# GpSimd's program order in a six-stage decoder kernel: when it issues scatters, triangle masks and normalisation steps

## What is computed

```python
x = _layernorm(x + _L0_attn_ref(x, ...))        # stage 1: linear attention by cumulative sums
x = _layernorm(x + _L0_xattn_ref(x, ctx, mask)) # stage 2: cross attention over 512 context tokens
x = _layernorm(x + _L0_ffn_ref(x, ...))         # stage 3: top-2 of 8 experts, sparse deltas on W
x = _layernorm(x + _L1_attn_ref(x, ...))        # stage 4: sliding window attention, 32 heads
x = _layernorm(x + _L1_xattn_ref(x, ctx, ...))  # stage 5: quantised cross attention, 16 heads
x = _layernorm(x + _L1_ffn_ref(x, ...))         # stage 6: top-6 of 64 experts
```

```python
rows = mask_idx // H
cols = mask_idx % H
vals = jnp.einsum('tk,tks->ts', rw, weighted[top_idx])
contrib = jax.ops.segment_sum((xg * vals).T, rows, num_segments=H)
out = xt @ W.T + contrib.T
```

## Time and profile before

| | |
|---|---|
| runs of the kernel | 472.28, 475.8 and 476.39 us, median 475.8 |
| profiled execution, span from first to last instruction | 473.8 us |
| TensorE matmuls busy | 388.1 us, 82% of the span |
| VectorE busy | 303.7 us, 64% |
| ScalarE busy | 215.5 us, 45% |
| GpSimd busy | 118.4 us, 25% |
| mean granted TensorE clock | 0.879 of full speed |

### The profile page before, as it was taken

The page is one execution under the profiler, slowest core; times in us unless marked ns, Lnnn a source line. Parts: engine busy times, 40 slices in busy tenths (PEclk is TensorE's granted clock), DMA queues, the critical chain, the costliest instruction groups (busy, mean ns, idle before and its releaser), DMA issues.

```text
span 473.8 us, 6810 instructions
## 1 busy us (share of the span) xinstructions
PE 388.1 (82%) x2387; PEld 225.7 (48%) x2387; DVE 303.7 (64%) x611; ACT 215.5 (45%) x551; POOL 118.4 (25%) x215
## 2 busy tenths in 40 slices
PE   5996969389987999999754867768676998999993
PEld 2645457244434566576532223333344544665572
DVE  4984498959624697878646979989871362132235
ACT  2664221272235765855214789899881311111100
POOL 8248646828460000000080111212110000000002
PEclk9989895779988899999985589998975698999997
DMA  8992110670000000000000999999982004011211
GB/s 244 318 361 25 1 2 1 223 310 1 0 1 0 1 3 0 2 1 1 2 0 13 265 169 172 155 163 173 131 162 51 0 0 143 24 44 49 63 44 44
DMA packets 75521, 39.84 MB, mean 84 GB/s; under 512 B 64160, under 2 KB 71264, under 8 KB 75040
## 3 DMA queue, kind: packets, MB, share of 16 engines
q1 hardware_dynamic: 73184, 39.35, 34.1%
q0 software_dynamic: 2304, 0.07, 1.4%
HBM read 21.58 MB, written 2.88 MB: 52 GB/s over the span
## 4 chain that ended last, share of the span: by engine, by line
PE 53%; DVE 15%; DMA 12%; ACT 10%; issue 5%; POOL 4%; SPq 0%; POOLq 0%; ACTq 0%; DVEq 0%
PE ps L762 27%; ACT area_b L692 7%; PE ps L1162 6%; DMA area_b<-area_b 6%; PE ps L945 5%; PE ps L956 5%; PE ps L975 3%; DMA area_a<-area_b 3%; POOL deltas L490 2%; PE ps L939 2%; DMA area_b<-deltas 1%; DVE area_a L1275 1%; DMA deltas<-entry_w,small 1%; ACT area_a L673 1%; DVE stats L1282 1%
## 5 line engine op out<-in xcount | busy, mean ns | idle before, releaser
L1535 DVE CUSTOM_DVE_ANT_0 area_a<-ps,zero,small 128x1024 f32<-128x1024 f32 x64 | 79.4, 1278 | 9.7 <-ACT area_b L692 5.0
L692 ACT ACTIVATE area_b<-area_a,small 128x1024 int16<-128x1024 f32 x64 | 73.0, 1142 | 11.3 <-DMA area_b<-area_b 5.9
L673 ACT ACTIVATE area_a<-ps,small 128x256 f32<-128x256 f32 (+1 forms) x128 | 51.9, 432 | 31.0 <-DVE small L1426 28.7
L459 POOL TENSOR_SCALAR var_eps<-meanvar 128x1 f32<-128x1 f32 x24 | 6.6, 273 | 225.3 <-DVE meanvar L1283 225.2
L762 PE MATMUL ps<-xT_odd,early 128*128 128x512 f32 x128 | 59.5, 613 | 0.0
L1054 PE MATMUL ps<-area_b 128*128 128x512 bf16 x128 | 45.0, 446 | 13.5 <-DVE small L1535 12.4
L1593 DVE TENSOR_TENSOR area_b<-ps,area_b 128x512 f32<-128x512 f32 x16 | 11.1, 691 | 55.7 <-ACT area_b L737 55.7
L1426 DVE TENSOR_REDUCE small<-ps 128x4 f32<-128x1024 f32 (+1 forms) x24 | 29.3, 1222 | 18.3 <-PE ps L945 18.1
L737 ACT ACTIVATE area_b<-ps 128x512 f32<-128x512 f32 x16 | 9.5, 596 | 67.2 <-PE ps L762 67.2
L762 PE MATMUL ps<-area_b,xT_even 128*128 128x512 f32 x64 | 31.1, 631 | 9.0 <-ACT area_b L650 9.0
L762 PEld LDWEIGHTS ps<-xT_odd,early 128*128 128x128 f32 x128 | 25.0, 197 | 27.1 <-issue 26.6
(11 more groups left out here) (265 smaller groups left out, 667.4 us busy)
## 6 DMA issues: line engine op xcount, KB each, us to landing
early<-in_w_up_dram SPq DMA_DIRECT2D x1, 4096.0 KB, 16.1
area_b<-gates_out SPq DMA_DIRECT2D x16, 256.0 KB, 3.0
deltas<-area_b SPq DMA_DIRECT2D x1, 2112.0 KB, 17.8
area_b<-deltas SPq DMA_DIRECT2D x2, 1024.0 KB, 5.9
area_a<-in_w_down_dram SPq DMA_DIRECT2D x1, 2048.0 KB, 8.5
early<-in_ctxT_dram SPq DMA_DIRECT2D x1, 1024.0 KB, 13.1
early<-in_ctx_dram SPq DMA_DIRECT2D x1, 1024.0 KB, 14.0
early<-in_w_qkv_dram SPq DMA_DIRECT2D x2, 384.0 KB, 5.1
```

The source lines that it names most:

```text
L673: a = act.activation(p1[:, n % 2, x * nk * P:(x + 1) * nk * P], scores1(n)[:, x * nk * P:(x + 1) * nk * P], ACT.Exp, bias=nmx1[:, n % 2, x ...
L692: act.activation(px[:, u % PX, :], sx[:, u % 3, :], ACT.Exp, bias=nbx[:, u:u + 1], accum_out=zx[:, i, h:h + 1]).then_inc(sem("px_ready"), 1)
L1535: dve.tensor_tensor_reduce(sx[:, u % 3, :], bank(2 * (u % 2), 2), zero[:].broadcast_to([P, B * M]), qsc[:, i, h:h + 1], LOWEST, ALU.add, A ...
```

## The change

Only GpSimd's stream is written in another order. Triangles 2 and 3 and scatters 4 to 7 move ahead of stage 1's deviations, right behind scatters 0 to 3. At the head of stage 2 there are now scatters 8 to 12; 13 goes behind the second deviation of stage 2 and 14 behind the third. One scatter, 15, is left for the start of stage 3, and the clearing of `kstack` goes behind it. The number of instructions is the same.

```diff
@@ -497,6 +497,10 @@
             linear_numerator(1)
             for j in range(GROUP):
                 scatter(j)
+            earlier_or_self(2)
+            earlier_or_self(3)
+            for j in range(GROUP, 2 * GROUP):
+                scatter(j)
@@ -520,16 +524,14 @@
             for n in range(1, STAGES + 1):
                 if n == 2:
-                    earlier_or_self(2)
-                    earlier_or_self(3)
-                    for j in range(GROUP, 3 * GROUP - 2):
+                    for j in range(2 * GROUP, 4 * GROUP - 3):
                         scatter(j)
                 if n == 3:
 
                     pool.wait_ge(sem("x_ready"), nth(2, TT - 1))
+                    for j in range(4 * GROUP - 1, SJ):
+                        scatter(j)
                     link(pool.memset(kstack, 0.0))
-                    for j in range(3 * GROUP - 1, SJ):
-                        scatter(j)
                     for k in range(GROUP):
                         stack_keys(k)
@@ -550,8 +552,8 @@
                 for i in range(TT - 1 if n == 5 else 0, TT):
                     inverse_deviation(n, i)
-                    if n == 2 and i == 1:
-                        scatter(3 * GROUP - 2)
+                    if n == 2 and 1 <= i <= 2:
+                        scatter(4 * GROUP - 4 + i)
```

## The result

| | before | changed |
|---|---|---|
| runs | 17 | 17 |
| median, us | 473.89 | 478.92 |
| lowest to highest, us | 469.69 to 476.74 | 473.02 to 483.79 |
| profiled execution, span | 473.8 | 477.3 |
| mean granted TensorE clock | 0.879 | 0.901 |

The ratio of the changed kernel to the one before is 1.0091, with a 95% interval of 1.006 to 1.0122: 4.3 us slower, between 2.8 and 5.8. The forecast was 2.5 us slower.

The account below looks back on a forecast made before the run. GpSimd was taken to set the pace at the ends of stages 1 and 2. 8.9 us of wait, less 1.9 for triangles, plus 1.4 for scatter 14, less 5.9 absorbed: 473.8 + 2.5 + 2.0 = 478.3 us, range 474.0 to 481.0.

Parts of the forecast that it names:

- Part 1: GpSimd ahead of stage 1's deviations: these start 8.9 us later, the early triangles give back 1.9, stage 2 shifts 7.0.
- Part 2: Scatters amid stage 2: the five at its head cost nothing, scatter 14 ahead of the fourth deviation costs 1.4 us.
- Part 3: After stage 2: deltas read back by 92.3 us, but ScalarE's key copies put the first y product at 98.2, 2.1 later.
- Part 4: Stage 3: of the 8.4 us shift, VectorE's waits for y absorb 5.2 and the slack ahead of y8 0.7.
- The rival of a clock fall: TensorE's y work: after new pauses the clock falls to 0.50 at y8, 2.05 us more, 480.3 us; 15%.
- The sum: Net effect through stage 3, up to y8 and every later stage: 8.4 - 5.2 - 0.7 = +2.5 us.
- nothing absorbed: Stage 3: VectorE's pass stretches beside GpSimd's key stacks until its 5.2 us are gone; 8.4 us reach the end, 484.2; 7%.

Follow-up runs that it names:

- scatter 14 late: Changed kernel with scatter 14 moved from between stage 2's third and fourth deviations to behind stage 2, with scatter 15; ratio to before 1.003.
- clearing first: Changed kernel with the clearing of the key stack put back ahead of scatter 15; ratio to before 1.0064.
- triangles only: Kernel before with one edit: triangles 2 and 3 ahead of stage 1's deviations; ratio to before 0.9906.
- head only: Kernel before with triangles 2 and 3 and scatters 4 to 7 ahead of stage 1's deviations, the rest as before; ratio to before 1.0075.
- scatters 4 to 7 back: Changed kernel with scatters 4 to 7 put back behind stage 1's deviations, at the head of stage 2; ratio to before 0.9963.
- fitted: Changed kernel with scatters 4 to 11 at stage 2's head, 12 behind its second deviation, 13 to 15 behind stage 2; ratio to before 0.992.

## Why the prediction was partly right

**Part 1, the queue ahead of stage 1's deviations: right.** The engine was to be free at 50.75 and was at 51.05, in a run whose rows lie 0.3 later from the start. The landing that scatter 4 waits for came 3.10 us after scatter 3's start; the forecast had 3.00 from a row. The "about 2.0 us" that the page "DMA: Bandwidth & Descriptors" of the Trainium skill has in its section on the anatomy of such a DMA would have been 1.1 short. Stage 2's first product shifted by 55.10 - 48.13 = 7.0 us, 6.7 without the 0.3, where 7.0 was forecast, with the clock at 0.50 from the transposes on.

**Part 2: right.** The first deviation of stage 2 waited 4.45 us for VectorE; scatter 14 held the fourth. x was ready at 81.51, forecast 81.7. With scatter 14 moved away, x came 1.4 us sooner behind the first scatter, which is the term.

**Part 3: right on deltas.** ScalarE's key copies ended at 95.4 (forecast 95.9), the first y product started at 97.6 (98.2), and deltas were not waited for. But this part said of the memset only that the key stacks lose nothing. It looked at GpSimd's own queue and not at what VectorE does beside it.

**Part 4, the absorption: the term that was mis-sized.** The text had VectorE work "without a gap from x to the end of the key quantiser" in the old 24.1 us. The road took 26.9, so the first use of a y came at 108.4 and not at 105.8. Of the 2.7 us, 1.9 are the one held instruction (2.96 instead of 1.07), and the rest is spread over the others beside GpSimd's key stacks. The runs show that the clearing's place is behind it: with the clearing on VectorE the road is 24.1 again, and with the clearing ahead of the last scatter the instruction takes 1.07 again, though the road only goes down to 26.0. The old trace had the smaller case of it: beside its memset at 73.34, the same instruction took 1.07 us, and that was in the 24.1. I had seen that row and not priced it, because I took the memset as moved and not as changed in what it meets.

**The rival of a clock fall** came true at y4 and not at y8. TensorE waited 3.46 us, not 1 to 2, the mean granted clock from 109 to 113 us was 0.62, and the eight matmuls of y4 and y5 took 5.37 us instead of 3.49. It cost nothing at y8. VectorE handed the bank back at 119.01 and y8 started at 119.16, 0.15 later; with scatter 14 late, where TensorE waited for VectorE ahead of y8, it was 0.15 too (116.60 and 116.75). So VectorE released y8, as the forecast had it.

```profile
109.00:113.00 4.00, 3.48 (x5) 1.65 (x6) 3.72 (x9) 0.00 (x0) 0.00 (x0) 0.62 0.00 0
```

```profile
119.16 0.67 PE L764 MATMUL ps<-area_b,xT_even 128*128 128x512 f32 x1
```

**The sum** at y8 was 2.5, and 5.5 in the profile. 2.7 of the difference is the longer road. The other 0.3 is the slack ahead of y8: the forecast had 0.7, from the hand-back at 113.11 to 113.85, but a y starts 0.15 after the hand-back that it waits for, and y8 stands at 113.69 in the old timeline, which leaves 0.4. The forecast had put the first product of stage 4 near 136 and called the sum wrong if it was not; it was at 138.94. The 4.3 of the timed runs, with its interval of 2.8 to 5.8, reaches to the 5.5; what of it came back lies in stage 4 and behind, and isn't an effect that I can show.

**The total was met by luck.** The forecast of 478.3 us lies close to the measured 478.92, with an effect that was too small on a base that was too high: it started from 475.8, the median of three runs, and the median of 17 is 473.89. From that base it would have said 476.4.

**The rival "nothing absorbed"** named the right place, VectorE's pass stretching, and its mark was met: the first use of a y came at 108.4, where it had "from 108 us on". Its cause was another one, the key stacks, and its size was not reached. It needed the stretch to take all of VectorE's 5.2 us of waits; the stretch took 2.7, about half. It had 7%.

## What to carry to other kernels

Work that is placed early to free a later stretch has to fit in a wait that is there: eight scatters fitted ahead of stage 2's first deviation, and four put ahead of stage 1's cost 9 us at once. Before a transfer's landing is brought forward, count on all engines what becomes the bound; here it was VectorE, 2.5 us behind. And a long instruction on GpSimd is to be priced by what VectorE issues beside it, as well as by its place in GpSimd's queue: one clearing of 1.8 us held an instruction of VectorE for up to 3.1.

## What the runs showed of the hardware

A TENSOR_SCALAR of VectorE that stood beside GpSimd's clearing waited until the clearing ended. It took 1.07 us in the four kernels where the clearing ran alone (before, clearing first, triangles only, head only). It took 2.96, 2.96, 2.45 and 3.14 us in the four where the clearing came right behind a scatter (changed, scatters 4 to 7 back, scatter 14 late, fitted). The TENSOR_REDUCE right ahead of it in the program was not held: it ran its usual 0.42 us at 73.65 in the kernel before, beside a clearing from 73.34 to 75.14. The second of the four long ones:

```profile
77.85 2.96 DVE L1324 TENSOR_SCALAR small<-small 128x16 f32<-128x16 f32 x1
```

In three of the four the instruction was issued clearly before the clearing's own row begins (82.34 against 82.88, 77.85 against 78.39, 77.14 against 77.74). The row at 82.34 ought to have been over by 82.51. So the hold begins ahead of the recorded start of the clearing, while the scatter in front of it is still running. The rows of GpSimd are rough, and what stands right behind a scatter is recorded as longer than it is alone (the clearing 2.38 us and 1.80), so how long ahead is not shown.

It is not only the clearing. In the kernel before, the first key stack stands right behind the last scatter, and VectorE's instruction there, 0.29 us at its shortest, took 0.79; it took 0.80 with the head only and 0.79 with the triangles only. A scatter with another scatter behind it held little: nothing at 80.62 with scatter 14 late (0.18 us), and a quarter of a microsecond at 83.25 in the kernel before (0.42), where the scatter too was longer than the others. No run put an instruction as long as the clearing, but of another kind, in its place.

```profile
83.25 0.42 DVE L1324 TENSOR_SCALAR small<-small 128x16 f32<-128x16 f32 x1
84.83 0.79 DVE L1337 TENSOR_SCALAR area_a<-area_a 128x256 f32<-128x256 f32 x1
```

```profile
82.39 1.77 POOL L490 DMA_INDIRECT deltas<-entry_w,small  x1 [0.30 <-issue]
85.48 1.36 POOL L510 TENSOR_TENSOR area_a<-area_a,small 128x256 f32<-128x256 f32 x1
```

The page "SBUF — State Buffer" of the Trainium skill, section on who interferes with whom, says that VectorE in a two-port mode and GpSimd take a shared pair of ports in turn, each for a whole instruction, and that the one that issues first has it. The rows agree in that the instructions that waited out the clearing are all of the kind with one tensor input (TENSOR_SCALAR), and each ends within 0.15 us of the clearing's end; in which mode they ran no row says. On who comes first they don't agree by their recorded starts: VectorE's instruction starts ahead of the clearing's row and still waits.

The granted clock after TensorE's pauses is not the same from one execution to the next. The first score product took 3.76 us in the changed kernel and 2.97 with the clearing first. The instructions ahead of it are the same in both, and the pause before the transposes was 10.1 and 11.5 us, so the longer pause had the shorter product. In the fitted order, after a pause of 2.2 us, the clock stayed at 1.00 and the product took 1.96; in the kernel before, whose triangle wait of 2.34 us stood right ahead of it, it took 3.76 at 0.50.
